# A perceiver layer on one core: head mixing moved from VectorE and GpSimd to TensorE, and the tail's order rewritten

## What is computed

```python
def _L0_attn_ref(x, Wq, Wk, Wv, Wo):
    q = (x @ Wq).reshape(b, n, H, DK)        # H = 16, DK = 32
    k = (x @ Wk).reshape(b, n, KH, DK)
    v = (x @ Wv).reshape(b, n, KH, DK)
    scores = jnp.einsum('bnhd,bnkd->bnhk', q, k)
    o = jnp.einsum('bnhk,bnkd->bnhd', scores, v)
    return o.reshape(b, n, d) @ Wo

x = x + _L0_xattn_ref(_layernorm(x), ctx_512, ...)
x = x + _L0_attn_ref(_layernorm(x), ...)
x = x + _L0_ffn_ref(_layernorm(x), ...)
```

## Time and profile before

| | us |
|---|---|
| median of 3 executions | 1244.73 (1244.6 to 1246.05) |
| profiled execution, its own time | 1240.12 |
| its span | 1238.3 |
| PE busy | 1114.0 (90%) |
| DVE busy | 985.4 (80%) |
| ACT busy | 704.3 (57%) |
| POOL busy | 578.0 (47%) |
| mean granted PE clock | 0.969 |

### The profile page before, as it was taken

The page is one execution under the profiler, slowest core; times in us unless marked ns, Lnnn a source line. Parts: engine busy times, 40 slices in busy tenths (PEclk is TensorE's granted clock), DMA queues, the critical chain, the costliest instruction groups (busy, mean ns, idle before and its releaser), DMA issues.

```text
span 1238.3 us, 23318 instructions
## 1 busy us (share of the span) xinstructions
PE 1114.0 (90%) x9080; PEld 838.0 (68%) x9080; DVE 985.4 (80%) x930; ACT 704.3 (57%) x1029; POOL 578.0 (47%) x698
## 2 busy tenths in 40 slices
PE   4999997999999999998999999999998869875688
PEld 3555556888888878876787788778787334334567
DVE  4887777899889989887888888888886089996933
ACT  1223236788878878876777777777775031113321
POOL 1993351765766444433344344343442077885200
PEclk9999998999999999999999999999999889987889
DMA  8443305999999999998999999999999200040000
GB/s 303 140 145 99 97 22 105 179 190 183 186 184 191 188 174 190 183 184 163 184 198 186 192 192 196 184 186 191 184 191 163 102 1 0 1 186 1 1 18 17
DMA packets 553990, 175.78 MB, mean 142 GB/s; under 512 B 535072, under 2 KB 541216, under 8 KB 553760
## 3 DMA queue, kind: packets, MB, share of 16 engines
q1 hardware_dynamic: 552272, 169.14, 73.4%
q10 hardware_dynamic: 1616, 5.24, 1.2%
HBM read 39.07 MB, written 1.05 MB: 32 GB/s over the span
## 4 chain that ended last, share of the span: by engine, by line
PE 64%; DMA 19%; DVE 8%; issue 4%; POOL 4%; ACT 2%; DVEq 0%; POOLq 0%; ACTq 0%; SPq 0%
DMA pt_both<-p_both 19%; PE ps_o L1180 7%; PE ps_o L1181 7%; PE ps_o L1184 6%; PE ps_s L1152 5%; PE ps_s L1153 4%; PE ps_s L1154 4%; PE ps_o L1214 3%; PE ps_o L1085 3%; PE ps_s L1060 3%; PE ps_t L1152 2%; POOL prod L517 2%; PE ps_s L1244 2%; PE ps_t L1153 2%; PE ps_t L1154 2%
## 5 line engine op out<-in xcount | busy, mean ns | idle before, releaser
L856 DVE SCALAR_TENSOR_TENSOR p_both<-prob,p_both 128x1024 f16<-128x1024 f32 x256 | 326.4, 1275 | 18.2 <-ACT p_both L597 17.7
L597 ACT ACTIVATE p_both<-prob 128x1024 f16<-128x1024 f32 x256 | 270.6, 1057 | 55.4 <-DMA pt_both<-p_both 37.0
L1180 PE MATMUL ps_o<-kn_hi,pt_both 128*128 128x128 f16 x2048 | 259.0, 220 | 31.6 <-DMA pt_both<-p_both 29.9
L1180 PEld LDWEIGHTS ps_o<-kn_hi,pt_both 128*128 128x128 f16 x2048 | 194.2, 98 | 107.1 <-issue 60.6
L1181 PE MATMUL ps_o<-kn_lo,pt_both 128*128 128x128 f16 x2048 | 256.7, 219 | 0.0
L864 DVE TENSOR_REDUCE nmax<-ps_s 128x1 f32<-128x1024 f32 x172 | 210.2, 1222 | 54.6 <-PE ps_s L1154 52.7
L606 ACT ACTIVATE prob<-ps_s,nmax 128x1024 f32<-128x1024 f32 x172 | 191.7, 1114 | 77.5 <-DVE nmax L864 77.0
L1181 PEld LDWEIGHTS ps_o<-kn_lo,pt_both 128*128 128x128 f16 x2048 | 201.2, 98 | 0.0
L1184 PE MATMUL ps_o<-kn_hi,pt_both 128*128 128x128 f16 x2048 | 156.6, 219 | 0.0
L1152 PE MATMUL ps_s<-kt_hi,q_hi 128*128 128x512 f32 x344 | 150.4, 437 | 4.9 <-DVE kt_lo L878 2.8
L1154 PE MATMUL ps_s<-kt_hi,q_lo 128*128 128x512 f32 x344 | 136.5, 397 | 0.0
(11 more groups left out here) (129 smaller groups left out, 2004.4 us busy)
## 6 DMA issues: line engine op xcount, KB each, us to landing
wgu_raw<-w_gu_dram SPq DMA_DIRECT2D x11, 512.0 KB, 7.5
wq_s<-wq_t_dram SPq DMA_DIRECT2D x16, 256.0 KB, 3.6
wot_s<-wo_t_dram SPq DMA_DIRECT2D x16, 256.0 KB, 2.8
kvr<-ctx_kv_dram ACTq DMA_DIRECT2D x4, 1024.0 KB, 13.7
pt_both<-p_both SPq DMA_TRANSPOSE x256, 4.6
kvr<-w_mix_dram SPq DMA_DIRECT2D x16, 256.0 KB, 3.4
wkcq_s<-w_kcq_dram SPq DMA_DIRECT2D x16, 192.0 KB, 3.0
wdn_raw<-w_dn_dram SPq DMA_DIRECT2D x1, 2816.0 KB, 9.1
```

What stands on the lines that cost most here:

```text
L597: nc.scalar.mul(p_hi(n), prob[:, n % 2, :], PSCALE).then_inc(hi_done, 1)
L856: nc.vector.scalar_tensor_tensor(out=p_lo(n), in0=prob[:, n % 2, :], scalar=PSCALE, in1=p_hi(n), op0=ALU.mult, op1=ALU.subtract).then_inc( ...
L1180: nc.tensor.matmul(o, pt_hi[:, k, :], kn_hi[b][:, keys], start=(k == 0), stop=False)
```

## The change

The mixing goes to PE. `mix_in` now multiplies with the weights as the standing operand and 128 tokens moving, so that q, k and v come out transposed, in 48 products of 128x128. ACT (q, v) and DVE (k) copy each bank in four instructions of 32 partitions so that the columns of one group of 8 tokens x 16 heads lie together and `d` on partitions 0 to 31. 16 transposes turn v back. For each of the 16 groups one product of 128x128 over 32 rows gives the scores of all pairs of (head, token); DVE multiplies four groups at a time with a mask that keeps pairs of the same token; one product with v (32 columns standing, 128 moving) gives the mixed values, and ACT copies them in four instructions of 32x128 per four groups straight to `mixT`, so `mix_out` has no transposes. The mask is made at the start from a periodic identity times itself. The tail's PSUM use is one list, `TAIL`, of 106 items on eight banks in turn; three semaphores count it (`full`, `act_free`, `dve_free`). The order changes too: two context tiles come first, the mixing of a tile stands in PE's list, and gate and up of the first pair comes after all mixing.

```diff
@@ PE @@
+            pe.wait_ge(period_ok, 2)
+            nc.tensor.matmul(ps_o[:, 0, 0:P], period, period, start=True, stop=True).then_inc(mask_mm, 1)
...
+            def empty(item):
+                k = TAIL.index(item)
+                if k >= 8:
+                    before = TAIL[k - 8]
+                    pe.wait_ge(act_free if before[0] in ACT_TAKES else dve_free, FREE[before])
+                elif k >= 6:
+                    pe.wait_ge(o_used, NQT)
+                else:
+                    pe.wait_ge(exp_done, NCHUNK)
+                return bank(item)
...
             def mix_in(t):
-                for m in range(3):
-                    for c in range(DC):
-                        last = nc.tensor.matmul(ps_s[:, m, :], ynT[:, t % 2, c, :],
-                                                wmix[:, (m * DC + c) * D:(m * DC + c + 1) * D],
+                for m, name in enumerate(("q", "k", "v")):
+                    o = empty((name, t))
+                    for g in range(4):
+                        for c in range(DC):
+                            w = (m * DC + c) * D + g * P
+                            last = nc.tensor.matmul(o[:, g * P:(g + 1) * P], wmix[:, w:w + P], ynT[:, t % 2, c, :],
...
+            def mix_values(t):
+                pe.wait_ge(act_free, FREE["v", t])
+                o = empty(("vt", t))
+                for g in range(NG):
+                    last = nc.tensor.transpose(o[:, g * DK:(g + 1) * DK], vT[0:DK, g, :],
+                                               ident[0:DK, 0:DK])
+            def mix_scores(t, j):
+                for i in range(4):
+                    g = 4 * j + i
+                    last = nc.tensor.matmul(o[:, i * P:(i + 1) * P], kT[0:DK, g, :],
+                                            qT[0:DK, g, :], start=True, stop=True)
+            def mix_weighed(t, j):
+                pe.wait_ge(dve_free, FREE["s", t, j])
+                for i in range(4):
+                    last = nc.tensor.matmul(o[0:DK, i * P:(i + 1) * P], vtok[:, t % 2, 4 * j + i, :],
+                                            same[:, j % 2, i, :], start=True, stop=True)
+            def mix_heads(t):
+                mix_values(t)
+                mix_scores(t, 0)
+                mix_scores(t, 1)
+                mix_weighed(t, 0)
+                mix_scores(t, 2)
+                mix_weighed(t, 1)
+                mix_scores(t, 3)
+                mix_weighed(t, 2)
+                mix_weighed(t, 3)
...
             context_out(0)
+            context_out(1)
             turn_norm("x", 0)
             mix_in(0)
+            context_out(2)
+            mix_heads(0)
+            turn_norm("x", 1)
+            mix_in(1)
+            mix_out(0)
+            context_out(3)
+            mix_heads(1)
+            turn_norm("x", 2)
+            mix_in(2)
+            mix_out(1)
+            mix_heads(2)
+            turn_norm("x", 3)
+            mix_in(3)
             mix_out(2)
             turn_norm("f", 0)
             turn_norm("f", 1)
+            mix_heads(3)
+            mix_out(3)
             gate_up(0)
             down(0)
             down(1)
+            turn_norm("f", 2)
             turn_norm("f", 3)
             gate_up(1)
@@ ACT @@
+            act.wait_ge(mask_mm, 1)
+            nc.scalar.copy(mask[:, :], ps_o[:, 0, 0:P]).then_inc(mask_ok, 1)
...
+            def heads(item, dst):
+                act.wait_ge(full, FULL[item])
+                for a in range(4):
+                    last = nc.scalar.copy(by_head(dst, a), of_head(item, a))
+            def mixed(t, j):
+                act.wait_ge(full, FULL["o", t, j])
+                src = bank(("o", t, j))[0:DK, :].rearrange("p (g h a s) -> p g h a s", g=4, h=4, a=4)
+                for a in range(4):
+                    dst = mixT[a * DK:(a + 1) * DK, 4 * (t % 2):4 * (t % 2) + 4, j * 32:(j + 1) * 32]
+                    last = nc.scalar.copy(dst.rearrange("p h (g s) -> p g h s", g=4), src[:, :, :, a, :])
...
             ctx_columns(0)
+            ctx_columns(1)
             normalise(("x", 0))
+            norm_columns(0)
             shift_down()
+            heads(("q", 0), qT)
             normalise(("x", 1))
+            heads(("v", 0), vT)
             ctx_columns(2)
+            values(0)
+            for j in range(4):
+                mixed(0, j)
+            norm_columns(1)
...
@@ DVE @@
+            def keys_of_heads(t):
+                dve.wait_ge(full, FULL["k", t])
+                for a in range(4):
+                    last = nc.vector.tensor_copy(by_head(kT, a), of_head(("k", t), a))
+            def same_token(t, j):
+                dve.wait_ge(full, FULL["s", t, j])
+                nc.vector.tensor_tensor(same[:, j % 2, :, :], bank(("s", t, j)).rearrange("p (g s) -> p g s", g=4),
+                                        mask[:, :].unsqueeze(1).to_broadcast([P, 4, P]), ALU.mult).then_inc(dve_free, 1)
...
+            layer_norm(("x", 0))
+            layer_norm(("x", 1))
+            keys_of_heads(0)
+            layer_norm(("x", 2))
+            for j in range(4):
+                same_token(0, j)
+            keys_of_heads(1)
+            layer_norm(("f", 0))
+            layer_norm(("x", 3))
...
@@ POOL @@
+            nc.gpsimd.memset(period, 0.0).then_inc(period_ok, 1)
+            pool.wait_ge(period_ok, 1)
+            nc.gpsimd.affine_select(out=period.rearrange("p (h s) -> p h s", s=8),
+                                    in_=period.rearrange("p (h s) -> p h s", s=8), compare_op=ALU.not_equal, fill=1.0,
+                                    base=0, pattern=[[0, P // 8], [-1, 8]], channel_multiplier=1).then_inc(period_ok, 1)
...
-            for t in range(NT - 1):
-                mix_qk(t)
-                norm_root(("x", t + 1))
-                mix_v(t)
...
+            for norm in NORMS[1:]:
+                norm_root(norm)
@@ lists @@
+TAIL = (_context(0) + _context(1) + _mix_in(0) + _context(2) + _mix_heads(0) + _mix_in(1) + [("mo", 0)] + _context(3)
+        + _mix_heads(1) + _mix_in(2) + [("mo", 1)] + _mix_heads(2) + _mix_in(3) + [("mo", 2), ("f", 0), ("f", 1)]
+        + _mix_heads(3) + [("mo", 3)] + _gate_up(0) + [("down", 0), ("down", 1), ("f", 2), ("f", 3)] + _gate_up(1)
+        + [("down", 2), ("down", 3)])
```

More of the change, by code:

```diff
@@ L49 @@
 DK = D // H
-HG = 4
+NG = P // 8
 EPS = 1e-5
@@ L648, in normalise @@
                 act.wait_ge(nmr_ok, k + 1)
-                if k >= 2:
-                    act.wait_ge(tr_done, max(BANKS.index(NORMS[i]) for i in range(k) if NORMS[i][1] % 2 == t % 2) + 1)
+                if t % 2 == 0 and k == 0:
+                    act.wait_ge(mask_ok, 1)
+                before = [FULL[m] for m in NORMS[:k] if m[1] % 2 == t % 2]
+                if before:
+                    act.wait_ge(full, max(before))
                 nc.scalar.activation(yn[:, t % 2, :], xres[:, t, :], ACT.Identity, bias=nmr[:, t:t + 1],
@@ L894, in layer_norm @@
                 kind, t = norm
-                n = OUTS.index(("out", t) if kind == "x" else ("mix", t))
+                item = ("out", t) if kind == "x" else ("mo", t)
                 dve.wait_ge(x_again, 16)
-                dve.wait_ge(acc_done, n + 1)
-                nc.vector.tensor_tensor(xres[:, t, :], ps_o[:, n % 2, :], xres[:, t, :], ALU.add).then_inc(acc_used, 1)
-                dve.wait_ge(acc_used, n + 1)
+                dve.wait_ge(full, FULL[item])
+                nc.vector.tensor_tensor(xres[:, t, :], bank(item), xres[:, t, :], ALU.add).then_inc(dve_free, 1)
+                dve.wait_ge(dve_free, FREE[item])
                 nc.vector.bn_stats(stats[:, t, :], xres[:, t, :]).then_inc(st_ln, 1)
@@ L1014, in _ @@
+            layer_norm(("f", 2))
+            norm_low(0)
+            norm_low(1)
+            for j in range(4):
+                same_token(3, j)
+            layer_norm(("f", 3))
+            dve.wait_ge(wdn_in, 16 * 3)
+            for j in range(HC):
                 gate_up(0, j)
-                hidden_low(0, j - 1)
+                if j:
+                    hidden_low(0, j - 1)
             hidden_low(0, HC - 1)
-            norm_low(2)
-            layer_norm(("f", 3))
             finish(0)
@@ L1081, in q_absorbed @@
                 pe.wait_ge(g_ok, h + 1)
-                if not first:
+                if first:
+                    pe.wait_ge(mask_ok, 1)
+                else:
                     pe.wait_ge(qabs_ok, h)
@@ L1229, in _, with turn @@
                 weighed_keys(n)
+            def empty(item):
[5 more added lines that the diff above has]
+                    pe.wait_ge(o_used, NQT)
+                else:
+                    pe.wait_ge(exp_done, NCHUNK)
+                return bank(item)
+            def turn(item, src):
+                o = empty(item)
+                for k in range(4):
+                    last = nc.tensor.transpose(o[:, k * P:(k + 1) * P], src(k), ident[:, :])
+                last.then_inc(full, 1)
@@ new lines, in context_out @@
```

(11 more changed lines are left out.)

347 lines of the change are left out of this document (124 added, 223 removed).

## The result

The changed kernel takes 1212.3 us (median of 4 executions, 1210.16 to 1217.81) where the kernel before takes 1244.66 (1242.26 to 1246.05): ratio 0.9749, 95% interval 0.9712 to 0.9785, 32 us less. The forecast was 1216 in a range of 1203 to 1240. The profiled execution of the changed kernel is its longest, 1217.81, with a span of 1216.0; so its stages are good for durations, and the comparison of times rests on the medians.

What follows compares the result with a forecast made beforehand. The tail was taken as bound by DVE and POOL mixing in turn with PE, afterwards by PE. 38.4 us saved, less 7 for clock and 3 for drains, gave 28.4: profiled 1211.7, median 1216, range 1203 to 1240.

Steps and rivals of the forecast that it cites:

- rival (e): In the tail, DVE or ACT remain the bound through in-order waits: each tile 6 to 7 us more, 1240; chance 0.03.
- The sum: Tail steps on PE added up at the high clock: end at 1196.0 against 1234.4, 38.4 us less.
- late start of tile 2's context: Context copies queue behind ACT's copies of v, so tile 2's context product starts 1.5 us late.
- wait at `mix_out(3)`: The last output projection waits 1.75 us for ACT's last copies, then takes 3.4.
- down as before 12.1: The last down projections at the tail's end, taken at 12.1 us as in the kernel before.
- The clock: Granted clock falls after PE waits at six tail spots, 1.7 us each; ends 0 and 10, 7 us taken.
- the gap at 1145: Between first gate and up and the first down matmul: 1.95 us, one of six spots for clock loss.
- rival (c): The mixing runs at the low clock: 7.8 us a tile, 31 in all, 1247; half of it 1231; chance 0.13.
- The drains: In mixings, changes between 128-row and 32-row or 32-column products cost 0.15 us each; ends 0 and 8, 3 taken.
- Rival (d): In mixings, loads can't run under products in the same 32 partitions: 9.9 us a tile, 40 in all, 1256; chance 0.06.
- Rival (b): Head copies in runs of eight elements cost 1.6 times: 9 to 10 us, 1226; chance 0.12.
- rival (a): In the tail, everything warm and no drains: 38 us less, 1206; chance 0.06.

Runs made afterwards that it cites:

- e0: The changed kernel run again, unaltered: 1210.4 us, ratio 0.9697 to the kernel before.
- e1: Changed kernel with tile 1's context product moved behind the turn and projection of tile 0: 1224.9 us, ratio 0.9806 to the kernel before.
- e3: Changed kernel with the 16 small value transposes per mixing replaced by four full-size ones of other data (values wrong): 1204.2 us.
- e5: Changed kernel with the 16 small value transposes of each mixing issued twice: 1220.6 us.
- e2: Changed kernel with 12 projection products of 512 columns per tile, not 48 of 128 (result wrongly laid out): 1215.4 us.
- e4: Changed kernel with output projections of tiles 1 and 2 behind the second score group of mixings 2 and 3: 1216.4 us, ratio 0.9786 to the kernel before.
- e6: Changed kernel with the next norm's turn and its copy ahead of the mixing, tiles 0 to 2: 1205.3 us, ratio 0.9698 to the kernel before.
- e11: The changed kernel run once more, unaltered, beside the later kernels on one chip: 1213.4 us, ratio 0.9775 to the kernel before.
- e10: e9 with the last output projection behind gate and up's first chunk, two weight shifts and a norm moved: 1199.2 us, ratio 0.9642 to the kernel before.
- e9: Changed kernel with early turns, down by chunk, and first score groups apart, right behind the projections: 1193.2 us, ratio 0.9601 to the kernel before.

## Why the prediction was right

What bounds the new tail and what its steps cost was right. That the total came within 1.5 us on the tail and 3.7 on the median is in part luck: errors of opposite sign cancel once between the sum and the clock, and once in the step to the median.

**The bound.** Right: with mixing on TensorE, PE is busy 234.8 of 247.7 us, and rival (e), DVE or ACT as the bound, is out by the windows (61.1 and 89.2 us). Per tile DVE has 4.48 us in mixing 0 or 1, 2.74 in a projection and 1.72 for a norm under a context product, 8.9 together, beside an estimate of 9.1.

**The sum.** The warm steps came out close: context 15.5 (forecast 15.5), projection 10.8 (10.6), late start of tile 2's context 1.4 (1.5), mixing 9.0 (9.1), turn with its wait 2.0 (2.3), wait at `mix_out(3)` 1.1 (1.75), gate and up 21.3 (21.4), gap 1.98 (1.95), down 0 and 1 10.4 (10.3), the turns of f2 and f3 2.9 (3.2). Inside the mixing the 16 small transposes take 1.0 and not 1.8. The eight groups take 7.96 (1066.53 to 1074.49) where 8 x 0.88 + 0.3 = 7.3 was forecast, with the changes of kind priced apart. With low clock left out on both sides (1.7 us of it stood inside "down as before 12.1") the forecast was 239.2 - 1.7 + 3 = 240.5, and 236.4 was measured: 4.1 too much. Of that 3.5 lie in the four mixings and 1.7 in the turns behind three of them and the wait at `mix_out(3)`; the projections had 0.9 too little, and small items make up the rest.

**The clock.** The term was right, its place wrong, and its size too small: 11.3 us (2 x 4.8 and 1.7) beside an allowance of 7 and the 1.7 inside the 12.1. The 2.6 us missing here and the 4.1 too much above leave the 1.5. I had put the loss behind the waits at the turns, at `mix_out(3)` and at the gap at 1145. In the profile of the changed kernel none of these is followed by a low clock. It came behind the last gap, which the forecast had inside "down as before". Of the nine profiles that keep both gaps it came behind the last one in five (changed, e0, e1, e3, e5; not e2, e4, e6, e11) and behind the first in one (e5). The losses lay in the mixings themselves, which is rival (c), and its sign showed: a clock of 0.63 across two mixings. It is true for two of four, at 4.8 us each and not 7.8, because the clock falls only 3 us into the mixing and the first groups run fast; so it cost 9.6 us and not the 31 of its full form, nor the half of that.

**The drains.** Allowance 0.15 a change, 3 us in all, measured about 0.1 a change, so 2.8 for 28: 0.98 to 1.09 between starts where the kind changes, 0.90 and 0.97 where it doesn't. The trace agrees in the sign with the Trainium skill, "TensorEngine Tiling (Array Packing)", Key Properties, that a change of tiling mode drains TensorE; the size is small.

**Rival (d)**, the mechanism of the other side, is out: eight score instructions over the same 32 rows take 0.97 us from start to start, 0.12 each, with their loads inside. The rule of the Trainium skill, "TensorE: Matmul & The Clock Gate", Part 3, that a load overlaps only with a matmul of another row group, isn't borne out for 32 rows either. **Rival (b)** is out: four mixed copies take 1.05 us, 0.26 each (0.31 had been taken, 0.5 feared).

**The median.** The forecast for the profiled execution was 1211.7, and it took 1217.81. Its tail is 1.5 us shorter than forecast, but starts at 964.4 where the profile before has 956.8, 7.7 later, although the code ahead of the tail is the same but for the mask. I had taken that part as fixed; over all fourteen profiles the tail starts between 956.8 (the kernel before) and 966.4 (e10). What moves it wasn't looked into; e11 and e0, the same kernel, have 959.1 and 961.8. Then I carried over 4.6 us from profile to median, and the profile after lies 5.5 above its median. So the start of the tail was 7.7 too early, the step to the median 10.1 too long and the tail 1.5 too long; together that is about the 3.7 us between 1216 and 1212.3, and that it is so little is luck. In e0 the two executions with little low clock, 1202.75 and 1205.40, are near the 1206 of rival (a).

## What to carry over

Where small products take the place of vector work, reckon the granted clock as a term of its own: price the block at full clock and at the low one, take several profiles, and compare them only after their low stretches are set apart. Once TensorE is the bound, list its waits by place and ask for each which independent step of its own queue could stand ahead of it; here two edits of that kind removed 9.5 us of waits and shortened the tail by 10.7 us at full clock, and they added up because each wait had its own place. The medians differ by 17.5 us; compare traces before the edits are given all of that. A step that is moved away may have been a cover: look up whose evictions ran beneath it.

## What the runs showed that I had not expected

- The clock falls while TensorE is busy without a gap: of the 40 mixings of the ten profiles whose head is unchanged or only lengthened (all but e3, e9 and e10), 17 were cold. In 16 of them the fall came 2.6 to 3.7 us behind the first small transpose (in e4 once at 0.7, behind a wait of 2.4). A warm one takes 9.0 us, a cold one of unchanged work 13.6 to 14.6. What decides which one it meets stays open. Wide products ahead (e2) or inside (e4) don't keep the clock up, nor does a break in the run (e9), and twice the small transposes (e5) didn't bring more falls. With full-size transposes in their place none of four was cold, once. DMA traffic doesn't decide it: mixing 1 of the changed kernel was warm beside 333 GB/s and mixings 2 and 3 cold beside 1 or less.
- A transpose of 32 x 32 costs 0.06 us (16 in 1.0, 32 in 2.0), half of a 128-column fp32 instruction's 0.11.
- Wide products of 512 columns may end a low stretch early, which two cases don't prove: in e4 it lasted 6.8 and 3.4 us, with output projections inside, in the other cold mixings 10.2 to 17.1. The longest (e0, e1, e2) ran on past the mixing, under a projection of 128-column products.
